# Keys and values on seven directions a head, a nine-row first chunk, and a new table of steps

## The reference

```python
# stage L0: three residual steps of two 3x3 convolutions
for _ in range(3):
    t = relu(conv(x, w1) + b1)
    x = x + (conv(t, w2) + b2) / 3
x = relu(x)
# stage L1: linear attention over the 4096 pixels, 8 heads of 8 channels
q, k, v = split(einsum('oc,bchw->bhwo', qkv_w, x).reshape(B, N, 8, 24)...)   # 1x1 projection
k, v = ln(k, kln_w, kln_b), ln(v, vln_w, vln_b)      # mean and std (ddof 1) over a head's 8 channels
o = einsum('bhnd,bhde->bhne', q, einsum('bhnd,bhne->bhde', k, v) / N)
u = einsum(o2_w, gelu(einsum(o1_w, o + x))) + x
out = gelu(u)
```

## Time and profile before

| | |
|---|---|
| median of 3 runs | 1303.31 us |
| profiled execution | 1304.89 us |
| its span, first to last instruction | 1303.1 us |
| TensorE matmuls busy | 1188.0 us, 91% |
| VectorE busy | 1085.5 us, 83% |
| ScalarE busy | 597.4 us, 46% |
| mean granted TensorE clock | 0.967 |

### The profile page before, as it was taken

The page is one execution under the profiler, slowest core; times in us unless marked ns, Lnnn a source line. Parts: engine busy times, 40 slices in busy tenths (PEclk is TensorE's granted clock), DMA queues, the critical chain, the costliest instruction groups (busy, mean ns, idle before and its releaser), DMA issues. The chain is left out here.

```text
span 1303.1 us, 40508 instructions
## 1 busy us (share of the span) xinstructions
PE 1188.0 (91%) x18613; PEld 805.4 (62%) x18613; DVE 1085.5 (83%) x1425; ACT 597.4 (46%) x642; POOL 91.1 (7%) x119
## 2 busy tenths in 40 slices
PE   6989999999999999999999999999999999785845
PEld 2546766577556766676566875676665875445432
DVE  3658888899888998899988997989978998987563
ACT  0212324454455626544455625554455625544573
POOL 2010110001010100101000100101000110110000
PEclk9989999999999999999999999999999999897876
DMA  7430330315061513515061422515061330430221
GB/s 131 91 68 1 69 68 2 68 36 102 18 150 33 102 36 99 101 36 102 2 164 35 86 52 70 129 35 102 2 163 36 69 69 34 100 68 2 82 51 65
DMA packets 87130, 88.95 MB, mean 68 GB/s; under 512 B 70320, under 2 KB 70320, under 8 KB 86960
## 3 DMA queue, kind: packets, MB, share of 16 engines
q0 software_dynamic: 13824, 51.91, 21.0%
q1 hardware_dynamic: 72496, 33.86, 10.3%
q10 hardware_dynamic: 640, 0.59, 0.3%
HBM read 17.66 MB, written 16.78 MB: 26 GB/s over the span
## 5 line engine op out<-in xcount | busy, mean ns | idle before, releaser
L956 PE MATMUL ps<-xs,w_t 64*64 64x512 f32 x4608 | 519.0, 594 | 10.2 <-DMA xs<-dx 6.3
L982 PE MATMUL ps<-v,fw 64*64 64x256 f32 x6912 | 398.9, 380 | 5.9 <-ACT m L552 4.1
L956 PEld LDWEIGHTS ps<-xs,w_t 64*64 64x64 f32 x4608 | 255.6, 134 | 224.1 <-issue 173.9
L982 PEld LDWEIGHTS ps<-v,fw 64*64 64x64 f32 x6912 | 302.2, 133 | 98.3 <-issue 18.4
L524 ACT ACTIVATE t<-ps,b_col 128x1024 f32<-128x1024 f32 x64 | 72.3, 1129 | 260.4 <-PE ps L956 204.9
L494 POOL DMA_DIRECT2D xs<-dx x96 | 83.4, 965 | 1154.3 <-DVE dx L829 1144.6
L722 DVE TENSOR_TENSOR q<-t 128x2112 f32<-128x2112 f32 x48 | 113.2, 2357 | 28.3 <-ACT t L524 15.4
L989 PE MATMUL ps<-v,sw 64*64 64x256 f32 x2304 | 134.4, 376 | 1.7 <-ACT t L524 1.7
L989 PEld LDWEIGHTS ps<-v,sw 64*64 64x64 f32 x2304 | 116.4, 132 | 21.5 <-issue 10.4
L554 ACT ACTIVATE m<-ps 128x1024 f32<-128x1024 f32 x80 | 82.2, 1028 | 65.6 <-PE ps L982 37.1
L836 DVE TENSOR_REDUCE rstd<-g 128x128 f32<-128x1024 f32 x64 | 77.1, 1216 | 38.7 <-ACT g L606 38.7
(11 more groups left out here) (108 smaller groups left out, 1115.4 us busy)
## 6 DMA issues: line engine op xcount, KB each, us to landing
xs<-dx POOLq DMA_DIRECT2D x96, 528.0 KB, 6.1
xs<-in_x SPq DMA_DIRECT2D x64, 256.0 KB, 5.1
out<-y SPq DMA_DIRECT2D x32, 512.0 KB, 3.1
q<-in_L_conv_w ACTq DMA_DIRECT2D x2, 144.0 KB, 6.1
v<-in_L_conv_w ACTq DMA_DIRECT2D x2, 144.0 KB, 7.3
b_col<-in_L_conv_b ACTq DMA_DIRECT2D x4, 0.2 KB, 6.1
y<-in_L_conv_qkv_w SPq DMA_DIRECT2D x4, 16.0 KB
y<-in_L_conv_o_w SPq DMA_DIRECT2D x4, 16.0 KB
```

Source lines behind the costliest of these rows:

```text
L956: last = mm(to[CH * side:CH * side + CH, BANK * p:BANK * p + BANK], w1_t[half, tap, :], tile[half, rows, c:c + COLS], start=tap == 0, stop ...
L982: last = mm(to[CH * i:CH * i + CH, at:at + SPAN], fw[rows, product, c, :], from_t[rows, tiles, place, i, c:c + COLS], start=c == 0, stop=c ...
```

## The change

Keys and values are projected onto seven orthonormal directions in the space that is orthogonal to the constant vector, instead of eight centred channels: `kvw` has 112 columns, PROJECT's matmuls write 4 x 112 columns a bank, ScalarE copies and squares 896 elements and writes the copies in runs of 7 words, VectorE sums squares over 7. `centre_map` turns the seven directions back. The chunks end at rows 9, 16, 25 and 32, and block 0 waits for the first only. One of the two copies of w1 is loaded by SP's queue, ahead of x. All tables have new places. Of them, those lines that are named later:

```diff
-CHUNK_ROWS = 8
-CHUNKS = ROWS // 2 // CHUNK_ROWS
+CHUNK_ENDS = (0, 9, 16, 25, 32)
+CHUNKS = len(CHUNK_ENDS) - 1
...
 CONV_PLACES = (
...
-        (SPREAD, CONV1, 0, 1): 10.04, (SPREAD, CONV1, 1, 0): -3.38, (SPREAD, CONV1, 1, 1): -2.33,
+        (SPREAD, CONV1, 0, 1): 8.4, (SPREAD, CONV1, 1, 0): -2.14, (SPREAD, CONV1, 1, 1): -1.64,
-        (MERGE, CONV1, 0, 1): 18.22, (MERGE, CONV1, 1, 0): 9.4, (MERGE, CONV1, 1, 1): 12.5,
+        (MERGE, CONV1, 0, 1): 16.43, (MERGE, CONV1, 1, 0): 10.08, (MERGE, CONV1, 1, 1): 11.47,
-        (MERGE, CONV1, 2, 0): 38.38, (MERGE, CONV1, 2, 1): 39.26,
-        (RECTIFY, CONV0, 1, 1): 38.28, (RECTIFY, CONV0, 2, 1): 27.49,
+        (MERGE, CONV1, 2, 0): 38.87, (MERGE, CONV1, 2, 1): 39.38,
+        (RECTIFY, CONV0, 1, 1): 40.68, (RECTIFY, CONV0, 2, 1): 26.09,
...
-        (SPREAD, CONV0, 1, 1): 26.06, (SPREAD, CONV0, 2, 1): 19.16, (SPREAD, CONV1, 0, 0): 8.88,
+        (SPREAD, CONV0, 1, 1): 23.98, (SPREAD, CONV0, 2, 1): 16.98, (SPREAD, CONV1, 0, 0): 6.48,
...
 LATE = {
-    (PIXELS, 0): -0.84, (PROJECT, 0): 1.3, (PROJECT, 1): 2.26, (PIXELS, 1): 2.29, (PROJECT, 2): 3.94,
-    (NORMALISE, 2): 8.18, (NORMALISE, 3): 8.75, (PIXELS, 2): 10.9, (PIXELS, 3): 11.22, (PROJECT, 4): 11.38,
-    (OUTER, 0): 11.65, (OUTER, 1): 11.97, (OUTER, 2): 14.28, (PROJECT, 5): 14.66, (OUTER, 3): 15.43,
-    (FOLD, 3): 29.59, (UP, 0): 30.46, (RELU, 1): 30.75, (UP, 1): 31.94, (DOWN, 0): 32.25, (FINISH, 0): 32.31,
+    (PIXELS, 0): -0.61, (PIXELS, 1): 0.21, (PROJECT, 0): 1.17, (PIXELS, 2): 2.38, (PROJECT, 1): 2.86,
+    (NORMALISE, 1): 7.13, (PIXELS, 3): 7.46, (NORMALISE, 2): 7.56, (NORMALISE, 3): 7.74, (OUTER, 0): 9.18,
+    (OUTER, 1): 9.62, (RELU, 0): 9.63, (PROJECT, 4): 10.36, (OUTER, 2): 10.91, (OUTER, 3): 12.44,
+    (PROJECT, 5): 12.97, (PROJECT, 6): 14.64, (PROJECT, 7): 16.36, (DEVIATION, 1): 21.44, (INVERT, 1): 23.24,
+    (NORMALISE, 4): 23.25, (RELU, 1): 23.53, (NORMALISE, 5): 23.68, (NORMALISE, 6): 23.76, (NORMALISE, 7): 23.86,
...
 LAST = {
-    (PROJECT, 4): 18.56, (NORMALISE, 1): 19.86, (NORMALISE, 2): 19.91, (OUTER, 0): 20.35, (NORMALISE, 3): 21.23,
-    (FOLD, 3): 36.85, (UP, 0): 37.47, (RELU, 1): 38.4, (DOWN, 0): 38.53, (UP, 1): 39.2, (FINISH, 0): 39.53,
+    (PIXELS, 3): 21.17, (NORMALISE, 1): 21.39, (OUTER, 0): 21.62, (PROJECT, 4): 21.86, (NORMALISE, 2): 23,
+    (RELU, 1): 34.99, (FOLD, 3): 36.8, (UP, 0): 37.94, (DOWN, 0): 38.18, (FINISH, 0): 38.37, (UP, 1): 38.65,
...
 FINAL = {
-    (NORMALISE, 1): 61.4, (NORMALISE, 2): 61.84, (PIXELS, 3): 62.09, (PROJECT, 4): 62.29, (PROJECT, 5): 62.43,
-    (OUTER, 0): 62.56, (NORMALISE, 3): 62.74, (RELU, 0): 62.77, (PROJECT, 6): 62.93, (OUTER, 1): 63.81,
-    (FINISH, 1): 74.95, (DOWN, 0): 75.63, (UP, 2): 77.06, (DOWN, 1): 77.47, (DOWN, 2): 77.47, (UP, 3): 77.71,
-    (FINISH, 2): 80.56, (FINISH, 3): 83.38, (DOWN, 3): 83.83,
+    (PIXELS, 3): 52.11, (NORMALISE, 1): 52.71, (NORMALISE, 2): 58.82, (NORMALISE, 3): 58.83, (RELU, 0): 62.49,
+    (PROJECT, 4): 64.15, (PROJECT, 5): 64.28, (OUTER, 0): 65.13, (OUTER, 1): 67.82, (PROJECT, 6): 67.96,
+    (FINISH, 0): 74.63, (DOWN, 1): 75.89, (UP, 2): 76.13, (FINISH, 1): 76.97, (DOWN, 2): 77.72, (UP, 3): 79.08,
+    (FINISH, 2): 79.68, (DOWN, 3): 82.13, (FINISH, 3): 83.33,
...
+            sp.dma_start(w_raw[0][:, 0:CH * K * K], w1.rearrange("o c y x -> o (c y x)")).then_inc(w_in[0], 16)
...
-            for copy in range(2):
-                act.dma_start(w_raw[0][:, CH * K * K * copy:CH * K * K * (copy + 1)],
-                              w1.rearrange("o c y x -> o (c y x)")).then_inc(w_in[0], 16)
+            act.dma_start(w_raw[0][:, CH * K * K:2 * CH * K * K], w1.rearrange("o c y x -> o (c y x)")
+                          ).then_inc(w_in[0], 16)
...
-                    nc.scalar.activation(kv[:, k % 4].rearrange("p i j t c -> p (i j t c)"), ring_ps[SLOT[a, *s]],
-                                         ACT.Copy)
+                    taken = ring_ps[SLOT[a, *s]].rearrange("p (i e) -> p i e", i=2)[:, :, 0:4 * FREE]
+                    nc.scalar.activation(
+                        kv[:, k % 4].rearrange("p i j t (h d) -> p i (j t h) d", d=HD)[:, :, :, 0:LAST_D],
+                        taken.rearrange("p i (g d) -> p i g d", d=LAST_D), ACT.Copy)
...
-                        for c in ((0, 1), (2,), (3,), ())[b]:
+                        for c in ((0,), (1, 2), (), (3,))[b]:
...
-                            at = BANK * p + P * j
+                            at = BANK * p + FREE * j
-                                last = mm(ring_ps[SLOT[a, *s]][columns, at:at + P],
+                                last = mm(ring_ps[SLOT[a, *s]][columns, at:at + FREE],
```

More of the change, by code:

```diff
@@ L153 @@
     {
[L154 to L159, removed]
@@ L171 @@
-    {
-        (SPREAD, CONV0, 1, 1): 26.06, (SPREAD, CONV0, 2, 1): 19.16, (SPREAD, CONV1, 0, 0): 8.88,
[L173 to L178, removed]
+        (SPREAD, CONV0, 1, 1): 10.05, (SPREAD, CONV0, 2, 1): 18.27, (SPREAD, CONV1, 0, 0): -23,
@@ new lines @@
+        (SPREAD, CONV1, 0, 1): -19.26, (SPREAD, CONV1, 1, 0): -12.95, (SPREAD, CONV1, 1, 1): -0.3,
+        (SPREAD, CONV1, 2, 0): 30.77, (SPREAD, CONV1, 2, 1): 32.34,
+        (MERGE, CONV0, 1, 1): 20.25, (MERGE, CONV0, 2, 1): 27.73, (MERGE, CONV1, 0, 0): -19.19,
+        (MERGE, CONV1, 0, 1): 5.61, (MERGE, CONV1, 1, 0): 9.4, (MERGE, CONV1, 1, 1): 11.26,
+        (MERGE, CONV1, 2, 0): 36.68, (MERGE, CONV1, 2, 1): 36.96,
+        (RECTIFY, CONV0, 1, 1): 41.12, (RECTIFY, CONV0, 2, 1): 28.46,
+    },
@@ L194 @@
+    (OUTER, 4): 24.05, (OUTER, 5): 24.3, (OUTER, 6): 24.41, (OUTER, 7): 27.79, (FOLD, 0): 28.23, (FOLD, 1): 29.37,
+    (FOLD, 2): 29.54, (FOLD, 3): 29.61, (UP, 0): 30.09, (UP, 1): 31.73, (FINISH, 0): 32.68, (DOWN, 0): 32.89,
+    (DOWN, 1): 33.91, (FINISH, 1): 34, (UP, 2): 34.52, (DOWN, 2): 36.33, (UP, 3): 37.16, (FINISH, 2): 37.36,
+    (FINISH, 3): 37.7, (DOWN, 3): 37.91,
 }
 LAST = {
-    (PIXELS, 0): -0.48, (PIXELS, 1): -0.38, (PROJECT, 0): 9.54, (PROJECT, 1): 11.73, (PROJECT, 2): 12.45,
-    (PIXELS, 2): 13.02, (PROJECT, 3): 14.43, (INVERT, 0): 15.69, (DEVIATION, 0): 17.11, (NORMALISE, 0): 17.26,
@@ L207 @@
+    (UP, 2): 39.39, (FINISH, 1): 41.7, (DOWN, 1): 41.7, (FINISH, 2): 41.7, (DOWN, 2): 41.7, (UP, 3): 41.9,
     (FINISH, 3): 41.9, (DOWN, 3): 41.9,
@@ L418, in load_chunk @@
             def load_chunk(a, c):
[L419 to L422, removed]
+                first, end = CHUNK_ENDS[c], CHUNK_ENDS[c + 1]
+                for rows in (slice(first, end), slice(ROWS - end, ROWS - first)):
+                    sp.dma_start(xs[a % X_RING][:, 1 + rows.start:1 + rows.stop, 1:COLS + 1],
+                                 pair_of(x, a)[:, rows, :]).then_inc(x_loaded[a % X_RING][c], 16)
+            sp.dma_start(w_raw[0][:, 0:CH * K * K], w1.rearrange("o c y x -> o (c y x)")).then_inc(w_in[0], 16)
             for c in range(CHUNKS):
```

74 lines of the change are left out of this document (45 added, 29 removed).

## The result

The changed kernel takes 1282.3 us (median of 4 runs, 1281.2 to 1283.3) against 1303.7 before (4 runs): 21.4 less, ratio 0.9836 with a 95% interval of 0.9812 to 0.986. The profiled execution took 1282.3, its span is 1280.6: 22.5 less than the span before.

| span, us | forecast | between the two profiles |
|---|---|---|
| start (first matmul of block 0) | 3.6 | 6.4 (13.8 to 7.4) |
| iterations 0 and 1 | 0 | 0.1 |
| iterations 2 to 7: projection 5.1, order 0 | 5.1 | 9.1 |
| iteration 8 | 1.7 | 0.5 |
| iteration 9 up to UP 0 | 3.7 | 4.6 |

What follows compares the result with a forecast made beforehand. TensorE was taken to bound iterations 2 to 6, chains through ScalarE and VectorE the last stretch. 5.1 + 3.6 + 0 + 1.7 + 3.7 + 3.0 = 17.1 us off 1304.9 gave 1287.8, range 1278 to 1299.

Steps and rivals of the forecast that it cites:

- The narrower projection: PROJECT with 112 instead of 128 columns: 0.107 us less on TensorE each, 48 times in iterations 2 to 7, 5.1 us.
- loads set the pace: PROJECT matmuls: unchanged weight loads set TensorE's pace, so fewer columns gain nothing; 1292.9 us, chance 0.07.
- The steady order: New places of steps in the steady pattern: nothing gained, nothing lost, 0 us (bounds -1.5 and +6).
- The start: Block 0 starts near 10.1 instead of 13.77 us, after earlier x and w1 loads: 3.6 us less (bounds 2 and 5).
- Iteration 8: SPREAD of x stands ahead of PROJECT 4's reduction on VectorE and starts some 2.5 earlier: 1.7 us taken (bounds 0 and 2.5).
- Gives part back: In iteration 8, UP 1 ahead of unit 3 waits for DOWN 0, returning part of the 2.5 us; 1.7 taken.
- Iteration 9 and the tail: Last iteration up to the first UP: 3.7 us less, 1.8 from RELU 0 moved; from UP 0 to the end: 3.0 less.
- the width isn't felt: Rival on PROJECT: the narrower width gains nothing because the loads set TensorE's pace; 1292.9 us, chance 0.07.
- the start gains nothing: Rival at the start: the ninth row's load lands with today's fourth, so no gain; 1291.4 us, chance 0.05.
- small waits come: Rival in the steady pattern: new waits of 1 to 1.5 us in each of six iterations; 1294 to 1297, chance 0.10.
- the ends did give back part: Rival in iterations 8 and 9: only their lower bounds come (0 + 1.8 + 1); 1293.4 us, chance 0.13.
- The slower rival: PIXELS 2 ahead of PROJECT 1: its DMA lands late, TensorE waits at PROJECT 2 in six iterations; 1312 us, chance 0.07.

Runs made afterwards that it cites:

- the 96 columns: The kernel before, with PROJECT's matmuls writing 96 of 128 columns for all pairs but the first; PROJECT's step 0.66 us, period 147.65 us (one run).
- The last two kernels with later DOWNs: Changed kernel, end of LAST as before, DOWN 3 later: one with DOWN 0 to 3, UP 2, UP 3 a unit later, 1278.2 us; one with DOWN 3 at 38.9, 1279.2.

## Why the prediction was right and where not

The time lies within the range, but the terms of the sum are off on both sides, and that they partly make up for one another is luck: the steady part was 4.0 too small, the start 2.8, of which 2.1 is a late start in the profile of before, and iteration 8 and the tail fell 2.3 short.

**The bound.** The step that failed is the first: that in iterations 2 to 6 an edit is worth what it takes from TensorE and other engines' steps are free. TensorE's busy share of 97% misled me; VectorE's 90% hid that it doesn't wait once in the 64 us up to FOLD 0. The run with a doubled reduction refutes it.

**The narrower projection.** Forecast 0.86 an iteration, measured 0.98 alone: nearly right for a wrong reason. By the loop, in the kernel before only PROJECT 0 to 3 count on TensorE (4 x 0.108) and the four later reductions on VectorE (4 x 0.136), together 0.98. I had put the reductions at nothing ("all that hides under TensorE"). In the new order all eight PROJECTs count on TensorE, 0.82. That "loads set the pace" would give nothing is refuted by the 96 columns. The rule weighed in the prediction (the Trainium skill, "TensorE: Matmul & The Clock Gate", section "Wait — 56ns, not 53.3ns?", no start within 25 ns of the last) asks at least 0.80 for a PROJECT here, however narrow; 0.77 and 0.66 for 32 matmuls are 24 and 21 ns each, so for these four-tile streams the measurement speaks against it.

**The steady order.** Forecast 0 with bounds of -1.5 and +6 in all; measured alone, 0.83 in each of the five iterations that repeat, some 5 in six: on the good side, and far outside the bound of 1.5. My walk looked for new waits and rightly found none. What it didn't ask is what an old wait costs (that before unit 2) and what the moved SPREAD does for VectorE's chain, since VectorE counted as hidden. Width and order together make the 9.1.

**The start.** Right mechanism, wrong size: 4.3 between the means. I interpolated the landing of x (9.9) between landings of one profile, which turned out the latest of its kind: its fourth load landed at 13.5, in the profile of the seven directions alone at 11.9. It came at 7.3, and the weights at 7.2, far inside my bound of 10.6. Against 12.4, the mean of the old start, 10.1 would have been 2.3, too little all the same. The same interpolation in the five other profiles of the old start gives 8.7 to 9.7, while in the six with the new one that load landed between 7.1 and 8.5: to go by the bytes on SP's queue was itself too slow a rule, and why is open.

**Iteration 8.** I took 1.7 and got 0.5, which is no more than the spread: 114.5 to 117.3 in seven profiles with the old `LAST`, 114.8 to 115.5 in the four with the new one. The front half gained more (68.6 to 66.0 up to OUTER 4; 1.9 between the means of these profiles). "Gives part back" was mis-sized: UP 1 ahead of unit 3 waits 1.73, worth 1.2 in all.

**Iteration 9 and the tail.** 4.6 for 3.7, within the spread of 0.9 between OUTER 4 and UP 0. RELU 0 alone is worth 0.8, not 1.8; with NORMALISE 3 and the rest of the order moved too the 1.8 comes. Up to the last gelu 2.8 of 3.0 came; then 0.9 went in the last store. Between the means of seven profiles with the old `FINAL` and seven with the new one the tail gained 2.3 (21.0 to 18.6).

**The rivals.** That the width isn't felt, that the start gains nothing and that small waits come are out by the runs above; the ends did give back part, 7.0 for 8.4. The slower rival didn't come in the changed kernel: in iterations 2 to 7 the DMA for PIXELS 2 lands 12.9 to 14.0 after the iteration's start (540.3, which is 13.5, was forecast). But it is near. ScalarE's timeline of the changed kernel, PIXELS 2 of iteration 4:

```profile
531.11 1.06 ACT L590 ACTIVATE y<-xs 128x1024 f32<-128x1024 f32 x1 [2.41 <-DMA xs<-dx]
```

There PIXELS 2 already starts with that landing, and PROJECT 2 starts 0.30 after the square it needs, where one that waits starts 0.14 after it. The rival came in the last two kernels with later DOWNs, where the DMA lands 15.1 to 16.6 after the iteration's start: its mechanism is real, and the margin is some 0.2 (an estimate from these two steps), not the 0.6 of my walk.
